# A gated cross-attention and mixture-of-experts block: the first batch on eight banks, xattn weights over a second queue, and q/k stacks filled from their own tiles

## The chip, the cores and the metric

The kernel runs on one core of one Trainium2 chip. A core has five engines that run side by side: TensorE (PE, matrix products, results in PSUM), VectorE (DVE), ScalarE (ACT), GpSimd (POOL) and SyncE (SP), which does nothing here but issue transfers. They meet only through semaphores. PSUM has eight banks of 128 x 512 fp32. The metric is the device time of one execution in microseconds; lower is better.

## The reference, cut to what matters

Four batches of 512 tokens with 256 features go through two parts: a gated cross-attention without a softmax (its result is a per-feature product), and a layer with a 16-head self-attention, a router and four experts.

```python
# part 1, per batch; xn = layernorm(x)
qh = (xn @ wq + bq) * gqw;  gq = sum_s(qh)
kh = (ctx @ wk + bk) * gq * gkw;  gk = sum_s(kh)
out = (ctx @ wv + bv) * gk + qh
x1 = x + tanh(g_xattn) * (out @ wo + bo)
# part 2; src = layernorm(x1)
q, k, v = src @ Wq + Bq, src @ Wk + Bk, src @ Wv + Bv          # 16 heads of 16
attn = softmax(q k^T / 4) v @ Wo + Bo
y = layernorm(src + attn) * ln1_g + ln1_b
e = floor(y @ router_w + router_b) mod 4                        # one expert per token
f = relu(y @ W1[e] + b1[e]) @ W2[e] + b2[e]
out = x1 + tanh(g_ffn) * layernorm_affine(y + f)
```

All is fp32. For accuracy q and k are kept as a high part and the rest ("lo"), and the scores are made from a stack of 48 rows per head: (q hi, q lo, q hi) against (k hi, k hi, k lo).

## The kernel before, in words

**Stages.** A lead does part 1 and the q, k, v projections of batch 0 (about 0 to 72 us). Then one loop over units u, 64 for each of the four batches, runs the attention of batch b and puts between its matmuls the part 1 and projections of batch b + 1 (up to about 420 us). A tail routes the tokens and runs the experts in slots of 256 tokens.

**A unit.** Unit u has one score matmul (`score`, L827, tile `sc`), one exponential on ACT (L549), and, 24 units ahead, one matmul for the row maxima (`score_for_maxima`, L818, tile `amax`) with a maximum on DVE (L686). Sixteen units are one group g of four heads of a batch; a batch has groups 0 to 3. Both matmuls read the stacks QS and KS. The first maxima matmul of group g waits for `stack_loaded[g]`; the first score of group g waits for the maxima of its sixteen rows, which DVE negates, splits and transposes (`mT`, L695) and SP moves through memory into two further rows of QS (`move_maxima`, L312 and L315).

**The queue of SP.** SP works through its transfers in program order, and each holds up those behind it until its own wait is over. For each batch `store_qk` (L291) writes the four q/k feature tiles HL to qk_dram, and `load_stack` (L303, L306) fills the stacks of one group from it with 12 transfers of 64 KB. A table `QUEUE` gives the unit at which each is written into SP's program: group 1 at -22, group 2 at -10, group 3 at 2, and the maxima of group g at 16 g - 8. Loads of batch b + 2 and of the expert weights (L352, L362) stand between. `load_stack` waits until the batch before has read the group's stacks.

**The lead.** The list `LEAD` gives its tasks: cT and xT (transposes of ctx and of the scaled x), gv (the sums behind gq and gk), Q, V, Y (part 1's three products), sT, q, k, v (part 2). All use two banks, side0 and side1, alternately; PE waits before it takes a bank until the task that had it before is evicted (`release`). Before the constants of DVE (L705 to L716) DVE waits for one semaphore `w_loaded` that counts all small loads and the four weights wq, wk, wv, wo (L700); PE's gv task waits for all twelve constants. Q is evicted to t1 (L607), and V combines it with gk (L612).

**Loads at the start.** SP issues everything: x, ctx, gates, the rows and columns, the four xattn weights (L330), then Wq, Wk, Wv and sixteen row pieces of Wo (L340), then x and ctx of batch 1. ACT waits for the gates, does one tanh, and then evicts cT. POOL waits for the gates too before it makes the first rstd.

Of the kernel before, what the change touches and what calls it, by code (L numbers as in the profile page):

```python
# [5 lines left out]
fp32 = mybir.dt.float32  # L6
# [8 lines left out]
def gated_block_kernel(nc, x, ctx, g_xattn, g_ffn, wq, bq, wk, bk, wv, bv, gqw, gkw, wo, bo,  # L15
# [23 lines left out]
    qk_dram = nc.dram_tensor("qk_dram", (4, 2, P, S), fp32, kind="Internal").ap()  # L39
# [6 lines left out]
    with es:  # L46
# [114 lines left out]
        pv = psum("pv", [P, 512])  # L161

# [6 lines left out]
        x_loaded, c_loaded, w_loaded, W_loaded, gates_loaded = sems("x_loaded c_loaded w_loaded W_loaded gates_loaded")  # L169
# [10 lines left out]
        m_loaded, qk_stored, stack_loaded = sems("m_loaded0 m_loaded1"), sems("qk_stored0 qk_stored1 qk_stored2 qk_stored3"), sems("stack0 stack1 stack2 stack3")  # L180
# [13 lines left out]
        W_LOADS, W_LOADS2 = 2 + 5 + 8 + 1 + 4, 3 + 16  # L194
        CONSTS = 12
# [12 lines left out]
        def rows_of(c, n):  # L208
# [19 lines left out]
                  -79: (("Q", 0),), -76: (("V", 0),), -73: (("Q", 1),), -71: (("V", 1),), -65: (("Y", 0),), -64: (("x1", 0),), -62: (("x1", 1),),  # L228
# [5 lines left out]
        QUEUE = {-117: ("load", 0), -42: ("store", 0), -39: ("store", 1), -37: ("store", 2), -34: ("store", 3),  # L234
                 -31: ("stack", 0), -22: ("stack", 1), -10: ("stack", 2), 2: ("stack", 3)}
# [12 lines left out]
        FIRST_PART = [("cT", 0), ("cT", 1), ("xT", 0), ("xT", 1), ("gv", 0), ("Q", 0), ("V", 0), ("Q", 1), ("V", 1), ("Y", 0), ("Y", 1)]  # L248
        LEAD = FIRST_PART + [("sT", 0), ("sT", 1), ("q", 0), ("q", 1), ("k", 0), ("k", 1), ("v", 0), ("v", 1)]

# [4 lines left out]
        def side_bank(task, i):  # L255

            return 1 if task in ("gv", "V") else 0 if task == "Q" else i % 2
# [8 lines left out]
        def release(task, n, b):  # L266
            return {"xT": (xT_done, b * 2 + n + 1), "cT": (cT_done, b * 2 + n + 1), "gv": (g4_done, b + 1),
                    "Q": (t1_done, b * 2 + n + 1), "V": (o_done, b * 2 + n + 1), "Y": (x1_done, b * 2 + n + 1),
                    "sT": (sT_done, b * 2 + n + 1), "q": (lo_done, b * 4 + n + 1), "k": (lo_done, b * 4 + n + 3),
                    "v": (v_done, b * 2 + n + 1), "O": (r_done, b * 2 + n + 1)}[task]  # L270

        def sp_program(sp):
# [11 lines left out]
            def store_qk(b, j):  # L284

                if j == 0:

                    for g in range(G):
                        wait(sp, stack_loaded[g], b * 192)
                sp.wait_ge(lo_done, b * 4 + j + 1)  # L290
                sp.dma_start(qk_dram[j, :, :, :].rearrange("h p n -> p h n"), HL[:, j, :, :].bitcast(fp32)).then_inc(qk_stored[j], 16)  # L291

            def load_stack(b, g, sides="qk"):

                if g == 0:
# [947 lines left out]
```

## Time and profile before

| what | value |
|---|---|
| median of 3 runs | 618.59 us (612.85, 618.59, 621.51) |
| the profiled execution | 614.73 us |
| its span, first to last instruction | 612.9 us |
| PE busy | 491.3 us, 80% of the span |
| DVE, ACT, POOL busy | 390.2, 244.7, 207.1 us |
| mean granted TensorE clock | 0.86 of 2.4 GHz |
| hardware transfers of the SP queue | 36432 packets, 38.84 MB |

The span is what the views show; the profiled execution's time is 1.8 us above it. "Idle before" in a row is the time that the engine waited right before the instruction, with what ended it. The granted clock is a share of 2.4 GHz; 0.5 is 1.2 GHz.

### The profile page before, as it was taken

The page shows a single profiled execution, that of the slowest core. Times are in us where ns is not written, and L with a number is a line of the kernel's source. Part 1 is how long each engine was busy: PE and PEld are TensorE (multiplying, and loading weights), DVE is VectorE, ACT ScalarE, POOL GpSimd, SP SyncE. Part 2 cuts the span into 40 slices and gives each one's busy share as a digit, 9 for nine tenths or more (in the row PEclk, how much of TensorE's full clock was granted, in tenths as well). Part 3 has the DMA queues.
Part 4 walks back from the last instruction along what each step waited for, and adds up shares of the span by engine and source line. Part 5 has one row for each costly group of instructions (what it writes and reads, how often), then busy time and mean ns, then how long its engine had stood idle before and what let it go on. Part 6 is the DMA issues. An engine that isn't in the chain of part 4 may idle for free. (4 is left out here: it accounts for less than half of the span.)

```text
span 612.9 us, 8282 instructions
## 1 busy us (share of the span) xinstructions
PE 491.3 (80%) x2528; PEld 281.8 (46%) x2528; DVE 390.2 (64%) x871; ACT 244.7 (40%) x482; POOL 207.1 (34%) x273
## 2 busy tenths in 40 slices
PE   2095769899898999999979798887239998988970
PEld 2053343434423433434332242223239988888970
DVE  2333446988768889679976779703885655655552
ACT  2000200465435456244654546447005555454440
POOL 3115110141101323403303248522144565455552
PEclk9997957999789899799995879655659999899995
DMA  5701844055334353632665840020021122111220
GB/s 145 164 0 38 282 129 67 3 198 180 84 78 121 114 196 93 139 102 58 152 187 140 176 112 3 2 70 1 1 68 35 51 61 58 45 52 40 64 54 25
DMA packets 41795, 55.00 MB, mean 90 GB/s; under 512 B 14367, under 2 KB 26143, under 8 KB 41760
## 3 DMA queue, kind: packets, MB, share of 16 engines
q1 hardware_dynamic: 36432, 38.84, 24.3%
q0 software_dynamic: 5328, 15.74, 8.5%
q8 instruction: 16, 0.26, 0.2%
q14 instruction: 19, 0.16, 0.1%
HBM read 37.51 MB, written 17.83 MB: 90 GB/s over the span
## 5 line engine op out<-in xcount | busy, mean ns | idle before, releaser
L549 ACT ACTIVATE probs<-sc 128x512 f32<-128x512 f32 x256 | 141.2, 595 | 178.0 <-PE sc L827 175.5
L686 DVE TENSOR_REDUCE mx<-amax 128x1 f32<-128x512 f32 x256 | 166.6, 677 | 58.9 <-PE amax L818 58.8
L827 PE MATMUL sc<-QS,KS 50*128 50x512 f32 x256 | 111.7, 520 | 15.3 <-ACT probs L549 12.2
L818 PE MATMUL amax<-KS,QS 48*128 48x512 f32 x256 | 110.4, 515 | 14.4 <-DMA KS<-qk_dram 8.5
L827 PEld LDWEIGHTS sc<-QS,KS 50*128 50x128 f32 x256 | 45.6, 210 | 121.2 <-issue 64.9
L818 PEld LDWEIGHTS amax<-KS,QS 48*128 48x128 f32 x256 | 43.9, 205 | 32.0 <-DVE mx L686 15.2
L1174 PE MATMUL amax<-W_hi,hid_hi 128*128 128x256 f32 x160 | 48.2, 301 | 3.8 <-DVE hid_lo L1074 3.6
L1174 PE MATMUL amax<-W_hi,hid_lo 128*128 128x256 f32 x160 | 46.6, 291 | 0.0
L1174 PE MATMUL amax<-W_lo,hid_hi 128*128 128x256 f32 x160 | 46.6, 291 | 0.0
L495 POOL TENSOR_TENSOR an<-av,rec 128x256 f32<-128x256 f32 x16 | 10.2, 637 | 106.8 <-DVE rec L675 106.7
L839 PE MATMUL pv<-probs,V1b 128*32 128x512 f32 x256 | 44.1, 769 | 1.4 <-ACT probs L549 1.2
L396 POOL TENSOR_SCALAR var_eps<-mv 128x4 f32<-128x4 f32 x12 | 2.8, 235 | 120.5 <-DVE mv L571 116.1
L758 PE MATMUL side<-xcT,w_first 128*128 128x512 f32 x64 | 40.8, 760 | 0.0
L839 PE MATMUL pv<-probs,V1a 128*32 128x512 f32 x256 | 39.6, 695 | 0.0
L991 ACT ACTIVATE t_a<-sc,b_col 128x256 f32<-128x256 f32 x40 | 19.3, 482 | 42.6 <-PE sc L1164 42.4
L930 POOL DMA_INDIRECT out_dram<-slot_z,ids_now x22 | 24.2, 1099 | 35.4 <-DVE slot_z L1114 32.0
L758 PE MATMUL side<-srcT,w_second 128*128 128x512 f32 x64 | 34.6, 667 | 0.8 <-ACT srcT L535 0.8
L1174 PEld LDWEIGHTS amax<-W_hi,hid_hi 128*128 128x128 f32 x160 | 32.0, 200 | 6.2 <-DVE hid_lo L1074 6.0
L1164 PE MATMUL sc<-slot_xT,W_hi 128*128 128x256 f32 x160 | 31.5, 292 | 1.5 <-DVE slot_xT L1068 1.5
L1174 PEld LDWEIGHTS amax<-W_lo,hid_hi 128*128 128x128 f32 x160 | 32.1, 200 | 0.0
L1174 PEld LDWEIGHTS amax<-W_hi,hid_lo 128*128 128x128 f32 x160 | 32.0, 200 | 0.0
L1074 DVE TENSOR_TENSOR hid_lo<-t_a,hid_hi 128x512 fp32r<-128x512 f32 x40 | 27.0, 690 | 6.0 <-ACT hid_hi L992 5.7
(180 smaller groups left out, 865.8 us busy)
## 6 DMA issues: line engine op xcount, KB each, us to landing
qk_dram<-HL SPq DMA_DIRECT2D x16, 512.0 KB, 4.6
QS<-qk_dram SPq DMA_DIRECT2D x96, 64.0 KB, 2.9
KS<-qk_dram SPq DMA_DIRECT2D x96, 64.0 KB, 3.0
W_sb<-in_L_ffn_W SPq DMA_DIRECT2D x8, 512.0 KB, 5.5
xc<-in_x SPq DMA_DIRECT2D x4, 512.0 KB, 3.6
xc<-in_ctx SPq DMA_DIRECT2D x4, 512.0 KB, 4.8
x_dram<-xc POOLq DMA_DIRECT2D x4, 512.0 KB, 3.4
res_dram<-t_a POOLq DMA_DIRECT2D x4, 512.0 KB, 5.4
```

Of the source, the lines that this page charges most:

```text
L495: nc.gpsimd.tensor_tensor(an[:, :, g % 2, :], av_v[:, :, 0:DH], rec[:, :].unsqueeze(2).broadcast_to([P, S // 32, DH]), ALU.mult).then_inc( ...
L549: nc.scalar.activation(probs[:, n % 8, c * 512:(c + 1) * 512], sc[c][:, :], ACT.Exp, scale=SCALE).then_inc(exp_done, 1)
L686: nc.vector.reduce_max(mx[:, to:to + 1], amax[m % 3][:, :], AX.X).then_inc(max_done, 1)
L758: last = nc.tensor.matmul(bank[:, :], w[:, k, c * P:(c + 1) * P], src[:, k, :], start=(k == 0), stop=(k == KD - 1))
L818: nc.tensor.matmul(amax[m % 3][:, :], QS[rows, pair, chunk * P:(chunk + 1) * P], KS[rows, pair, :], start=True, stop=True).then_inc(A_full, 1)
L827: nc.tensor.matmul(sc[c][:, :], KS[rows, pair, kc * P:(kc + 1) * P], QS[rows, pair, :], start=True, stop=True).then_inc(sc_full, 1)
L839: last = nc.tensor.matmul(pv[32 * hh:32 * hh + 32, :], V1[b % 2][:, kc, 8 * c + pair, :], probs[:, (2 * r + hh // 2) % 8, c * 512:(c + 1) ...
L930: nc.gpsimd.indirect_dma_start(out_rows, bass.IndirectOffsetOnAxis(ap=ids_now[:, a:a + 1], axis=0), slot_z[:, a, :], None, bounds_check=NT ...
L991: nc.scalar.activation(hid[:, q % 2, f % 2, :], hid_bank[f % 4], ACT.Relu, bias=bias)
L1074: nc.vector.tensor_tensor(low, hid[:, q % 2, :, :], high.bitcast(fp32), ALU.subtract).then_inc(hid_split, 1)
L1164: last = nc.tensor.matmul(hid_bank[f % 4], w, slot_xT[:, xp, k, :], start=((k, (xp, wp)) == steps[0]), stop=((k, (xp, wp)) == steps[-1]))
L1174: last = nc.tensor.matmul(amax[a][:, 0:D], (hid_hi, hid_lo)[xp][:, f, a * P:(a + 1) * P], w, start=(f == 0 and (xp, wp) == PARTS[0]), stop ...
```

## The change

- **Banks and order of the lead.** `LEAD` becomes cT, cT, V0, xT, xT, V1, gv, Q0, Q1, Y, Y and then sT, q, k, v; a table `LEAD_BANK` spreads batch 0 over all eight banks. V is now evicted first (gk V + C1 into oT), Q is added in place. Transposes of xT and sT wait tile by tile for their source.
- **Loads at the start.** ACT issues wv, wq, wk, wo and the two gates; SP the rest. `w_loaded` becomes seven semaphores. DVE needs only the rows gqw, gkw and the columns for its first six constants; the five that belong to part 2 are made after Q1. POOL's first rstd waits for gqw alone.
- **Stacks.** `qk_dram` and its stores are gone. `load_parts` copies from HL straight to the stacks: 6 transfers of 16 rows x 512 per side and feature tile, 24 of 32 KB per group in place of 12 of 64 KB. For group 0 of batch 0 SP issues q0, q1 and k0, and ACT issues k1. SP loads batch 1's x and ctx behind k0 now, ahead of the stacks of groups 1 to 3. ACT waits for all four groups of the batch before (no longer for the stores) when it overwrites HL.
- **Table of SP.** Group 0 at -39 (q) and -34 (k), group 1 at -22, group 2 at -6 (was -10), group 3 at 1 (was 2).
- Smaller: POOL's x1 store of batch 0 waits for all four src tiles and the constants.

The core of the diff:

```diff
-        FIRST_PART = [("cT", 0), ("cT", 1), ("xT", 0), ("xT", 1), ("gv", 0), ("Q", 0), ("V", 0), ("Q", 1), ("V", 1), ("Y", 0), ("Y", 1)]
+        LEAD = [("cT", 0), ("cT", 1), ("V", 0), ("xT", 0), ("xT", 1), ("V", 1), ("gv", 0), ("Q", 0), ("Q", 1), ("Y", 0), ("Y", 1),
+                ("sT", 0), ("sT", 1), ("q", 0), ("q", 1), ("k", 0), ("k", 1), ("v", 0), ("v", 1)]
+        LEAD_BANK = {"cT": (0, 1), "V": (4, 5), "xT": (2, 3), "gv": (6,), "Q": (7, 0), "Y": (1, 2),
+                     "sT": (3, 4), "q": (5, 6), "k": (7, 2), "v": (0, 1)}
...
-        QUEUE = {-117: ("load", 0), -42: ("store", 0), -39: ("store", 1), -37: ("store", 2), -34: ("store", 3),
-                 -31: ("stack", 0), -22: ("stack", 1), -10: ("stack", 2), 2: ("stack", 3)}
+        QUEUE = {-117: ("load", 0), -39: ("stack", (0, "q")), -34: ("stack", (0, "k")), -22: ("stack", (1,)), -6: ("stack", (2,)), 1: ("stack", (3,))}
...
-                sp.dma_start(qk_dram[j, :, :, :].rearrange("h p n -> p h n"), HL[:, j, :, :].bitcast(fp32)).then_inc(qk_stored[j], 16)
+            def load_parts(eng, b, g, side_of, c):
+                to = (QS, KS)[side_of == "k"]
+                for i, part in enumerate(((0, 1, 0), (0, 0, 1))[side_of == "k"]):
+                    at = 64 * c + DH * i
+                    for r in range(2):
+                        eng.dma_start(to[at:at + DH, 2 * g + r, :].bitcast(fp32),
+                                      HL[32 * g + DH * r:32 * g + DH * r + DH, c + 2 * (side_of == "k"), part, :].bitcast(fp32)).then_inc(stack_loaded[g], 16)
...
+            for side_of, c in (("q", 0), ("q", 1), ("k", 0)):
+                sp.wait_ge(lo_done, 1 + c + 2 * (side_of == "k"))
+                sp.wait_ge(stack_ready, 1)
+                load_parts(sp, 0, 0, side_of, c)
             load_batch(1)
...
         def act_program(act):
-            act.wait_ge(gates_loaded, 48)
+            for n, ap, s in (("wv", wv, wv_loaded), ("wq", wq, wq_loaded), ("wk", wk, wk_loaded), ("wo", wo, wo_loaded)):
+                act.dma_start(w_sb[n][:, :, :], ap.rearrange("(k p) n -> p k n", p=P)).then_inc(s, 16)
+            act.dma_start(gates[:, 0:1], g_xattn.partition_broadcast(P)).then_inc(gates_loaded, 16)
...
-            dve.wait_ge(w_loaded, W_LOADS * 16)
-            dve.wait_ge(gates_ready, 1)
+            dve.wait_ge(rows_s_loaded, 32)
+            dve.wait_ge(cols_loaded, 5 * 16)
```

The first place is PE in the lead of batch 0. Before, behind the transposes of cT, the rows are gv (xsum and csum), Q0, V0, Q1, V1, and Y:

```order
L753 MATMUL side1<-ident,xc 128x128 x4
L753 MATMUL side0<-ident,t_a 128x128 x4
L753 MATMUL side1<-ident,t_a 128x128 x4
L790 MATMUL side1<-xsum,w_first 128x1 x4
L790 MATMUL side1<-csum,w_first 128x1 x4
L758 MATMUL side0<-xcT,w_first 128x512 x2
L758 MATMUL side1<-xcT,w_first 128x512 x2
L758 MATMUL side0<-xcT,w_first 128x512 x2
L758 MATMUL side1<-xcT,w_first 128x512 x2
L766 MATMUL side0<-w_first,oC 128x256 x4
L766 MATMUL side1<-w_first,oC 128x256 x4
```

The same place after the change:

```order
L774 MATMUL side1<-ident,xc 128x128 x4
L779 MATMUL amax0<-xcT,w_first 128x512 x2
L774 MATMUL sc0<-ident,t_a 128x128 x4
L774 MATMUL sc1<-ident,t_a 128x128 x4
L779 MATMUL amax1<-xcT,w_first 128x512 x2
L811 MATMUL amax2<-xsum,w_first 128x1 x4
L811 MATMUL amax2<-csum,w_first 128x1 x4
L779 MATMUL pv<-xcT,w_first 128x512 x2
L779 MATMUL side0<-xcT,w_first 128x512 x2
L787 MATMUL side1<-w_first,oC 128x256 x4
L787 MATMUL sc0<-w_first,oC 128x256 x4
```

V0 and V1 (the two products that need ctx alone) moved ahead of gv, and no two tasks from V0 to Y0 share a bank.

The second place is SP in batch 1, from the maxima of group 0 (L312, L315) to those of group 1. Before, where the stack loads of group 3 lie between them and those of group 2 lie ahead:

```order
L303 DMA QS<-qk_dram 16x2x512
L306 DMA KS<-qk_dram 16x2x512
L312 DMA m_dram<-mT 4x32x32
L315 DMA QS<-m_dram 2x2x512 x2
L352 DMA W_sb<-in_L_ffn_W 128x1024
L303 DMA QS<-qk_dram 16x2x512
L306 DMA KS<-qk_dram 16x2x512
L303 DMA QS<-qk_dram 16x2x512
L306 DMA KS<-qk_dram 16x2x512
```

Ten more rows of L303 and L306 follow there, then:

```order
L303 DMA QS<-qk_dram 16x2x512
L306 DMA KS<-qk_dram 16x2x512
L352 DMA W_sb<-in_L_ffn_W 128x1024
L312 DMA m_dram<-mT 4x32x32
L315 DMA QS<-m_dram 2x2x512 x2
```

After the change (L310 and L313 are the maxima, L296 the stack pieces):

```order
L310 DMA m_dram<-mT 4x32x32
L313 DMA QS<-m_dram 2x2x512 x2
L345 DMA W_sb<-in_L_ffn_W 128x1024
L296 DMA QS<-HL 16x512 x12
L296 DMA KS<-HL 16x512 x12
L296 DMA QS<-HL 16x512 x12
L296 DMA KS<-HL 16x512 x12
L345 DMA W_sb<-in_L_ffn_W 128x1024
L310 DMA m_dram<-mT 4x32x32
L313 DMA QS<-m_dram 2x2x512 x2
```

Between the two moves of maxima stood 12 stack pieces and two weight loads; now 48 pieces and the same two loads do.

The third place is SP at the end of the lead, from the sixteen pieces of Wo to the first move of maxima, after the change:

```order
L335 DMA w_second<-in_L_ffn_Wo 16x256 x16
L296 DMA QS<-HL 16x512 x12
L296 DMA KS<-HL 16x512 x6
L286 DMA xc<-in_x 128x4x256
L288 DMA xc<-in_ctx 128x4x256
L296 DMA QS<-HL 16x512 x12
L296 DMA KS<-HL 16x512 x12
L296 DMA QS<-HL 16x512 x12
L296 DMA KS<-HL 16x512 x12
L296 DMA QS<-HL 16x512 x12
L296 DMA KS<-HL 16x512 x12
L310 DMA m_dram<-mT 4x32x32
```

Before, this place had x and ctx of batch 1, two stores, 6 pieces, two stores, 6 pieces, and 36 pieces for groups 1 to 3; now 18 pieces, x and ctx, and 72 pieces.

## Rows read from the trace of the kernel before

**Rows 1.** Stretch, busy us of PE, PEld, DVE, ACT, POOL, granted clock, DMA share, GB/s

```profile
180.00:260.00 80.00, 77.28 (x362) 33.04 (x360) 66.22 (x150) 39.50 (x74) 22.65 (x34) 0.91 0.44 127
```

**Rows 2.** Start, in order of time: start, us, engine, line, what, count, idle before

```profile
9.21 0.20 ACT L523 ACTIVATE tg<-gates 128x2 f32<-128x2 f32 x1 [7.20 <-DMA gates<-in_g_ffn]
...
24.54 0.88 DVE L705 TENSOR_SCALAR rows_bc<-rows_bc,tg 128x256 f32<-128x256 f32 x3 [12.11 <-DMA w_first<-in_L_xattn_wo]
...
30.85 1.84 PE L790 MATMUL side<-xsum,w_first 128*128 128x1 f32 x8 [16.34 <-DVE csum L591]
```

**Rows 3.** First batch, the same view

```profile
34.26 9.57 PE L758 MATMUL side<-xcT,w_first 128*128 128x512 f32 x16
...
43.87 0.75 DVE L612 SCALAR_TENSOR_TENSOR oC<-side,gk,t 128x512 f32<-128x512 f32 x1 [0.96 <-PE side L758]
...
52.45 2.19 DVE L628 TENSOR_SCALAR t_a<-xc,mv,rstd 128x256 f32<-128x256 f32 x4 [1.48 <-POOL rstd L398]
...
66.44 0.75 DVE L633 SCALAR_TENSOR_TENSOR HL<-side,cols,HL 128x512 fp32r<-128x512 f32 x1 [0.97 <-ACT HL L541]
...
71.71 1.40 DVE L567 BATCH_NORM_STATS2 stats<-xc 128x6 f32<-128x256 f32 x4
...
73.45 0.94 SPq L291 DMA_DIRECT2D qk_dram<-HL  x2
...
76.81 1.08 PE L753 MATMUL side<-ident,t_a 128*128 128x128 f32 x4 [4.30 <-DVE t_a L585]
77.80 2.65 SPq L306 DMA_DIRECT2D KS<-qk_dram  x6
...
82.34 0.79 PE L818 MATMUL amax<-KS,QS 48*128 48x512 f32 x2 [4.45 <-DMA KS<-qk_dram]
```

**Rows 4.** Stretch in which x and ctx land

```profile
2.00:5.00 3.00, 0.00 (x0) 0.00 (x0) 0.70 (x3) 0.01 (x1) 2.97 (x1) 1.00 0.98 338
```

**Rows 5.** SP's sixteen 16-row loads; landing times by transfer

```profile
20.86 7.51 SPq L340 DMA_DIRECT2D w_second<-in_L_ffn_Wo  x16
...
QS<-qk_dram SPq DMA_DIRECT2D x96, 64.0 KB, 2.9
...
xc<-in_x SPq DMA_DIRECT2D x4, 512.0 KB, 3.6
```

**Rows 6.** Maxima of the first group, and the first score

```profile
105.14 0.67 SPq L312 DMA_DIRECT2D m_dram<-mT  x1
107.18 1.29 SPq L315 DMA_DIRECT2D QS<-m_dram  x2
...
112.18 0.50 PE L827 MATMUL sc<-QS,KS 50*128 50x512 f32 x1
```

**Rows 7.** Waits of PE for the stack loads: us in total, times, longest

```profile
PE amax L818 <- DMA KS<-qk_dram: 8.5, 3, 4.5
```

**Rows 8.** Maxima of group 0 on SP; score of group 1, batches 1, 2, 3

```profile
180.53 0.55 SPq L312 DMA_DIRECT2D m_dram<-mT  x1
...
209.84 0.50 PE L827 MATMUL sc<-QS,KS 50*128 50x512 f32 x1
...
263.80 0.55 SPq L312 DMA_DIRECT2D m_dram<-mT  x1
268.14 1.26 SPq L315 DMA_DIRECT2D QS<-m_dram  x2
...
291.55 0.50 PE L827 MATMUL sc<-QS,KS 50*128 50x512 f32 x1
...
341.57 0.55 SPq L312 DMA_DIRECT2D m_dram<-mT  x1
...
348.17 0.49 PE L827 MATMUL sc<-QS,KS 50*128 50x512 f32 x1 [2.22 <-DMA QS<-m_dram]
...
367.14 0.47 PE L827 MATMUL sc<-QS,KS 50*128 50x512 f32 x1 [0.54 <-ACT probs L549]
```

**Rows 9.** Stretch behind a wait of PE of 2.8 us

```profile
323.00:340.00 17.00, 15.97 (x61) 4.55 (x60) 11.08 (x21) 7.56 (x14) 6.57 (x9) 0.51 0.64 125
```

More of the change, by code:

```diff
@@ L161, in gated_block_kernel @@
         pv = psum("pv", [P, 512])
+        BANKS = side + sc + amax + [pv]
         SEMS = {}
@@ L539, in side_work @@
                     act.wait_ge(qk_full, b * 4 + j + 1)
-                    wait(act, qk_stored[j], b * 16)
+                    for g in range(G):
+                        wait(act, stack_loaded[g], b * STACK)
+                    if b == 0 and j == 0:
+                        act.wait_ge(cols_loaded, 5 * 16)
                     nc.scalar.activation(HL[:, j, 0, :], bank[:, :], ACT.Identity, bias=cols[:, 3 + j // 2, i:i + 1]).then_inc(hi_done, 1)
@@ L552, in act_program @@
                 side_work(task, i, 0)
+            act.wait_ge(lo_done, 4)
+            act.wait_ge(stack_ready, 1)
+            for i, part in enumerate((0, 0, 1)):
+                for r in range(2):
+                    act.dma_start(KS[64 + DH * i:64 + DH * i + DH, r, :].bitcast(fp32), HL[DH * r:DH * r + DH, 3, part, :].bitcast(fp32)).then_inc(stack_loaded[0], 16)
             for u in range(BEGIN, END):
@@ L573, in side_work @@
             def side_work(task, i, b):
-                bank = side[side_bank(task, i)]
+                bank = BANKS[bank_of(task, i, b)]
                 if task == "x":
@@ new lines, in dve_program @@
+            side_work("cT", 0, 0)
+            side_work("cT", 1, 0)
+            dve.wait_ge(gates_ready, 1)
+            dve.wait_ge(bo_loaded, 16)
+            nc.vector.tensor_scalar(rows_bc[:, BO, :], rows_bc[:, BO, :], tg[:, 0:1], None, ALU.mult).then_inc(bo_ready, 1)
+            for task, i in (("gv", 0), ("V", 0), ("V", 1), ("Q", 0), ("Q", 1)):
+                side_work(task, i, 0)
+            later_constants()
+            side_work("Y", 0, 0)
+            for t in range(2):
+                side_work("x1", t, 0)
@@ L731, in dve_program @@
+            side_work("Y", 1, 0)
+            for t in range(2, TT + 1):
+                side_work("x1", t, 0)
+            for t in range(TT):
+                side_work("src", t, 0)
+            for v in V1:
+                nc.vector.memset(v[:, :, :, DH:2 * DH], 1.0).then_inc(v1_ready, 1)
+            for task, i in LEAD[LEAD.index(("q", 0)):]:
+                side_work(task, i, 0)
             for u in range(BEGIN, END + OVER):
@@ L748, in pe_program, with transposes @@
         def pe_program(pe):
-            before_side = [None, None]
-            def transposes(bank, src, c, full):
+            last_use = [None] * len(BANKS)
+            def transposes(bank, src, c, full, ready=None, b=0):
                 for t in range(TT):
+                    if ready is not None and c == 0:
+                        pe.wait_ge(ready, t + 1 + b * TT)
                     last = nc.tensor.transpose(bank[:, t * P:(t + 1) * P], src[:, t, c * P:(c + 1) * P], ident[:, :])
@@ L799, in side_work @@
                 elif task == "sT":
-                    pe.wait_ge(src_done, b * TT + TT)
-                    transposes(bank, t_a, i, sT_full)
+                    transposes(bank, t_a, i, sT_full, src_done, b)
                 elif task in "qk":
```

158 lines of the change are left out of this document (69 added, 89 removed), and 2 rows, old and new, of the table BLOCKS.

## The prediction

> **What bounds the kernel now.** I read the table of stretches first. In the attention loop PE is the bound: 77.28 us busy of 80, DVE 66.22, ACT 39.50 [rows 1]. Time that PE stands there is lost, and nothing gives it back. Then I read the timeline of the lead. It is a chain of waits instead: DVE stands 12.11 us until 24.54, for the last of the four weights in SP's queue, though its constants need none of them, and PE stands 16.34 us behind it, until gv at 30.85 [rows 2]. The end of the lead is a chain too: k0's low part is done at 66.44 + 0.75 = 67.2, its store goes out at 73.45, the loads of KS at 77.80, and the first maxima matmul starts at 82.34 [rows 3]. Last I read SP's queue, since the change doubles the stack transfers, and looked for what is queued behind them: x and ctx of the next batch, expert weights, and the maxima, on which PE's scores wait.
>
> **The front of the lead.** DVE's constants now wait for small loads only. PE has cT, V0, xT, V1 ahead of gv. ACT's tanh is at 9.21 [rows 2] and the two evictions of cT follow; the weights on the second queue share the transfer engines with x and ctx, so I place cT's end at 11. Eight transposes took about 1.9 us (four 1.08 at 76.81 [rows 3]; twice that is 2.2). The four tasks Q, V took 9.57 together, 2.4 each [rows 3]. So gv starts between 11 + 2.4 + 2 + 2.4 = 17.8 and about 20, since the first of them run at the low clock; I take 19. Against 30.85 that is 11.8 us. DVE's constants and sums took 6.3 us, 24.54 to 30.85 [rows 2], now less; they lie under V0 to V1 (11 to 19) if their loads land by 13, and each us later costs one. From gv to the last eviction of part 1 it now takes 43.87 + 0.75 - 30.85 = 13.8 [rows 2, 3], of which gv itself 34.26 - 30.85 = 3.4. With V already done it is 3.4, two products at 1.7 (the last step of the old chain, 0.96 + 0.75 [rows 3]) to 2.4, and one eviction: 7.7 (up to 9). Gain 6.1, together 17.9.
>
> The Trainium skill, DMA: Bandwidth & Descriptors, Issuing engines are not separate DMA queues, says that transfers of all issuing engines run on the same engines and a second issuer saves only issue time; that speaks against any gain from the second queue. The trace agrees: the stretch in which x and ctx land has share 0.98 at 338 GB/s [rows 4], full already. By it 1 MB of weights beside them makes ctx up to 3.1 us late, not the 1.5 us that my 11 holds, and the total would be 1.6 us higher.
>
> **From part 1 to the stacks.** Two of four statistics tasks slip in front of the second Y (0.7). The four src tiles took 2.19 from 52.45 while POOL worked beside them, and the transposes waited for all; tile by tile and with POOL held back I take 1.6 less. The q/k matmuls took their own time and no bank wait showed but small ones: 0.4. So k0's low part comes at 67.2 - 17.9 - 2.7 = 46.6 [rows 3]. POOL's held-back store of x1 is off this path, since SP asks for it only behind k0.
>
> SP issues a 16-row piece each 7.51 / 16 = 0.47 us [rows 5]. That is the nearest row to the new pieces, which also have 16 rows. k0's six pieces end at 49.4; x and ctx of batch 1 at 50.3; x lands 3.6 later [rows 5], at 53.0. ACT's six pieces of k1 (ready one product, 1.7 to 2.4, after k0) land by 49.0 + 2.8 + 2.9 = 54.7 [rows 5]. But in PE's order the first xT of batch 1 stands ahead of the first maxima, and from x's statistics to it took 76.81 - 71.71 = 5.1 [rows 3]; about the length of that xT is saved by its waiting tile by tile. So the first maxima is at 53.0 + 5.1 = 58.1. Before: 82.34. The chain through memory was 15 us behind k0, this one is 11.5, and **x of batch 1 is what is late next**, not the stacks.
>
> The first score was at 112.18 [rows 6], 29.8 behind the first maxima, so PE gets there at 88. SP: 72 pieces behind 50.3 end at 84.1, and only then the maxima move. That takes 2.0 for the store, 1.3 for the issue [rows 6], and a landing; in batch 3 it was 348.17 - 341.57 = 6.6 in all [rows 8]. I take 5.5 for it everywhere (bounds: 3.3, with no landing at all, and 6.6). The first score comes at 89.6, and the lead is worth **22.6 us**. A faster lead alone cannot better that, SP sets it.
>
> **In the loop.** PE's waits for KS, 8.5 in all with 4.5 the first, go in two later batches: the round through memory is gone, **gain 4.0** [rows 7]. Against it, between the maxima of group 0 and group 1 SP now has 48 pieces (48 x 0.47 = 22.6) where 12 stood. Group 1's maxima are needed by its first score:
> - batch 1: from 180.53 to 209.84 there are 29.3 us [rows 8]. Supply: the move of group 0, 3.3; 48 pieces and 2 weight loads, 23.5; the move of group 1, 5.5: 32.3. Late 3.0.
> - batch 2: 291.55 - 263.80 = 27.8 [rows 8]. Supply: 268.14 + 1.26 - 263.80 = 5.6, then 22.6, then 5.5: 33.7. Late 5.9.
> - batch 3: 367.14 - 341.57 = 25.6 [rows 8]. Supply 3.3 + 23.5 + 5.5 = 32.3. Late 6.7.
>
> That is **15.6 us lost**: PE's queue is in order, so all maxima and side matmuls behind that score stand too. If SP had no such queue ahead, the cost were nothing. The q eviction of ACT, which now waits for group 3's pieces, is covered: in batch 1 they have landed 3.3 + 23.5 + 2.9 = 29.7 behind 180.53, at 210.2, and q stands behind the first score of group 1 (209.84 plus its new wait). Group 2's pieces arrive within 1 us of their first use on both sides; I count nothing.
>
> A wait of 2.8 us was followed by 17 us at clock 0.51, with PE busy 15.97 [rows 9]; half speed costs at most 8.5 there. Two such waits go and three longer ones come. Bounds 0 and 8.5; I take **2 lost**, since the last batch runs partly on ACT.
>
> **The sum:** -22.6 - 4.0 + 15.6 + 2 = -9.0. The profiled execution's 614.73 becomes 605.7. It was 3.9 under the median 618.59; the same change on the median gives **609.6**, my number, 1.5% faster. The tail is not touched.
>
> **Rivals.**
> - *The group 1 waits don't come.* If SP issues pieces whose both ends are in SBUF faster, or the maxima are faster, only -22.6 - 4.0 or somewhat less is left: 592 to 596. It needs 15.6 / 3 = 5.2 us per batch, a piece at 0.36 in place of 0.47. Against it: six pieces of 64 KB took 2.65, 0.44 each [rows 3], so the pace hardly knows the size. For it: with the clock low PE needs the scores later. 0.18.
> - *The lead gives only half.* If ctx, gates and columns land late behind the weights, or the low clock covers V0 to gv, gv is at 23 or more; if x of batch 1 lands late among the stack pieces, a few more. With 12 instead of 22.6 it is 620. For it: the transfer engines are full [rows 4]. Against it: the wait for the weights alone was 12.11 [rows 2], and it is gone in any case. 0.16.
> - *Slower: copies within SBUF are slower than their issue.* 16 rows of 2 KB from the tile's partitions to the stack's, in one queue in order. If a piece holds the queue for more than its 0.47, SP's ring fills, and stacks and maxima are late in each group. 216 pieces lie on paths that bind (72, and 48 in three batches). 2% slower than 618.59 is 631; that takes 21 us more, 0.1 per piece, so it decides at 0.57 us per piece. At 0.8 it were 680. Against it: pieces of 64 KB, twice the bytes, landed in 2.9 [rows 5]. 0.08.
> - My forecast, with group 1's waits between 8 and 18 us: 0.58.
>
> **How the numbers follow.** A measurement tells 2% from no change, that is below 606.2 or above 631. My forecast's own range is 603 to 616; a third of it lies below 606.2: 0.20, with the first rival's 0.18 it is 0.38 faster. Slower 0.08. Same 0.54. The range goes from 593 to 621: it holds my forecast, half of the first rival and most of the second.
>
> **What would show it.** gv on PE near 19 us, k0's low part near 47, first maxima near 58, first score near 90 with a wait for QS from m_dram. SP without a gap from k0's pieces to about 84. In batches 1 to 3 a wait of PE for QS from m_dram at the first score of group 1, of 3, 6 and 7 us; no wait for KS. I am wrong if pieces do not go at 0.47, if those waits are under 2 us each, or if the clock falls for long after them.

## The result and the profile after

The changed kernel is slower: 668.12 us median (663.69 to 672.66, 4 runs) against 615.72 (608.94 to 621.51, 4 runs), a ratio of 1.098 with a 95% interval of 1.090 to 1.106. The profiled execution took 663.69 us with a span of 661.8. Forecast were 609.6 us and a range of 593 to 621; the true side had a chance of 0.08.

The lead did what it should up to k0. The timeline of the changed kernel, columns as in [rows 2]:

```profile
12.18 0.20 ACT L521 ACTIVATE tg<-gates 128x2 f32<-128x2 f32 x1 [6.48 <-DMA gates<-in_g_ffn]
...
20.28 0.95 PE L811 MATMUL amax<-xsum,w_first 128*128 128x1 f32 x8
...
45.82 0.75 DVE L640 SCALAR_TENSOR_TENSOR HL<-pv,cols,HL 128x512 fp32r<-128x512 f32 x1 [0.97 <-ACT HL L542]
...
60.05 1.94 PE L774 MATMUL side<-ident,xc 128*128 128x128 f32 x8 [9.82 <-DMA xc<-in_ctx]
...
63.65 0.80 PE L838 MATMUL amax<-KS,QS 48*128 48x512 f32 x2
...
106.09 0.79 PE L847 MATMUL sc<-QS,KS 50*128 50x512 f32 x1 [12.01 <-DMA QS<-m_dram]
```

gv starts at 20.28 (forecast 19, before 30.85 [rows 2]), k0's low part is done at 45.82 + 0.75 = 46.57 (forecast 46.6), the first maxima matmul is at 63.65 (forecast 58.1, before 82.34 [rows 3]). Then the gain is gone: the first score comes at 106.09 (forecast 89.6, before 112.18 [rows 6]), after 12.01 us in which PE stood for the maxima from m_dram. SP's queue over the same time shows why:

```profile
42.42 8.06 SPq L296 DMA_DIRECT2D QS<-HL  x12
50.58 3.73 SPq L296 DMA_DIRECT2D KS<-HL  x6
54.42 0.53 SPq L286 DMA_DIRECT2D xc<-in_x  x1
54.99 0.51 SPq L288 DMA_DIRECT2D xc<-in_ctx  x1
55.54 7.47 SPq L296 DMA_DIRECT2D QS<-HL  x12
...
93.71 7.54 SPq L296 DMA_DIRECT2D KS<-HL  x12
101.29 0.66 SPq L310 DMA_DIRECT2D m_dram<-mT  x1
```

SP has no gap from 50.58 on. Twelve pieces take 7.47 to 7.54 us here (7.87 once), **0.63 us a piece**, not the 0.47 that I took from Wo's pieces [rows 5]. The move of the maxima at 101.29 stands behind 72 of them. Before the 63.65 PE had already stood 9.82 us for ctx of batch 1, whose load SP reached only at 54.99, behind x.

The table of waits, for PE (us in total, times, longest):

```profile
PE sc L847 <- DMA QS<-m_dram: 38.6, 4, 12.0
...
PE amax L838 <- DMA KS<-HL: 25.5, 8, 5.6
```

Before, the loads of KS cost 8.5 us in three waits [rows 7] and the maxima 3.0 in two, the longer of 2.22 [rows 8]. Now it is 25.5 in eight and 38.6 in four. Four places carry 53 of these 64 us: the lead, and the stretch between the maxima of group 0 and the first score of group 1 in each later batch. The timeline there (L310 is the maxima's way out, the L838 rows are group 2's first maxima, the L847 rows group 1's first score):

```profile
177.14 0.60 SPq L310 DMA_DIRECT2D m_dram<-mT  x1
...
198.40 0.80 PE L838 MATMUL amax<-KS,QS 48*128 48x512 f32 x2 [4.26 <-DMA KS<-HL]
...
213.57 0.60 SPq L310 DMA_DIRECT2D m_dram<-mT  x1
...
219.46 0.79 PE L847 MATMUL sc<-QS,KS 50*128 50x512 f32 x1 [9.30 <-DMA QS<-m_dram]
...
296.63 0.80 PE L838 MATMUL amax<-KS,QS 48*128 48x512 f32 x2 [5.59 <-DMA KS<-HL]
...
316.52 0.79 PE L847 MATMUL sc<-QS,KS 50*128 50x512 f32 x1 [7.78 <-DMA QS<-m_dram]
...
392.27 0.80 PE L838 MATMUL amax<-KS,QS 48*128 48x512 f32 x2 [4.82 <-DMA KS<-HL]
...
406.73 0.61 SPq L310 DMA_DIRECT2D m_dram<-mT  x1
...
412.88 0.79 PE L847 MATMUL sc<-QS,KS 50*128 50x512 f32 x1 [9.53 <-DMA QS<-m_dram]
```

In batch 1 it is 219.46 - 177.14 = 42.3 us from one to the other, where the kernel before took 29.3 [rows 8]; PE stands 4.26 + 9.30 of it. In batch 2 the two waits are 5.59 and 7.78, in batch 3 4.82 and 9.53.

The transfer engines are not what is full. The first row is the stretch in which SP issues pieces and hardly anything else, the second the landing time of a piece:

```profile
60.00:95.00 35.00, 32.01 (x84) 16.58 (x84) 22.11 (x44) 2.57 (x6) 4.70 (x7) 0.67 0.22 51
...
QS<-HL SPq DMA_DIRECT2D x192, 32.0 KB, 2.0
```

DMA share 0.22 at 51 GB/s, and 2.0 us from issue to landing, less than the 2.9 of the pieces from memory, which carry 64 KB [rows 5].

Spans add up so. From the first score to the end it is 661.8 - 106.1 = 555.7, before 612.9 - 112.2 = 500.7: the loop and tail lost 55.0, the lead gained 6.1, together +48.9. The loop alone, from the first score to the last (columns as in [rows 1]; the first row is the kernel before), with the stretch behind the first score below it for each kernel:

```profile
112.18:417.90 305.72, 280.99 (x1293) 109.24 (x1292) 231.15 (x492) 154.07 (x284) 91.05 (x116) 0.87 0.41 111
106.09:467.90 361.81, 294.71 (x1292) 111.50 (x1292) 234.18 (x491) 154.21 (x284) 90.75 (x116) 0.79 0.28 76
...
112.00:129.00 17.00, 15.88 (x87) 6.67 (x85) 15.75 (x36) 11.38 (x21) 7.51 (x11) 1.00 0.10 34
106.00:123.00 17.00, 16.14 (x58) 5.66 (x58) 13.00 (x30) 7.62 (x14) 5.07 (x7) 0.50 0.01 3
```

The loop is 56.1 us longer. PE stands 67.1 us of it where it stood 24.7, and is busy 13.7 us longer with the same matmuls, at a granted clock of 0.79 for 0.87. Behind the wait of 12.01 us the clock is 0.50, and 58 matmuls keep PE busy for 16.14 us; in the kernel before 87 took 15.88.

### The profile page after: what moved, and what is told of

It is laid out like the page before. It is cut to its first block and busy times, and to the rows that moved or that the text cites. A ratio compares the mean times of both kernels' runs of the same rounds, so it can differ in the third digit from the quotient of the medians.

```text
span 661.8 us, 8466 instructions
## 1 busy us (share of the span) xinstructions
PE 500.3 (76%) x2528; PEld 279.4 (42%) x2528; DVE 392.8 (59%) x871; ACT 244.4 (37%) x482; POOL 206.9 (31%) x273
## 5 line engine op out<-in xcount | busy, mean ns | idle before, releaser
L847 PE MATMUL sc<-QS,KS 50*128 50x512 f32 x256 | 119.7, 556 | 51.3 <-DMA QS<-m_dram 38.6
L838 PE MATMUL amax<-KS,QS 48*128 48x512 f32 x256 | 115.0, 556 | 29.5 <-DMA KS<-HL 25.5
L847 PEld LDWEIGHTS sc<-QS,KS 50*128 50x128 f32 x256 | 49.4, 227 | 165.5 <-issue 73.3
L838 PEld LDWEIGHTS amax<-KS,QS 48*128 48x128 f32 x256 | 46.1, 223 | 43.8 <-DMA KS<-HL 28.2
L859 PE MATMUL pv<-probs,V1b 128*32 128x512 f32 x256 | 46.9, 815 | 1.2 <-ACT probs L550 1.2
L859 PE MATMUL pv<-probs,V1a 128*32 128x512 f32 x256 | 43.8, 764 | 0.0
L1012 ACT ACTIVATE t_a<-sc,b_col 128x256 f32<-128x256 f32 x40 | 19.3, 484 | 40.7 <-PE sc L1185 34.6
L1195 PEld LDWEIGHTS amax<-W_hi,hid_hi 128*128 128x128 f32 x160 | 30.5, 191 | 8.4 <-DVE hid_lo L1095 7.9
L779 PE MATMUL side<-xcT,w_first 128*128 128x512 f32 x52 | 31.6, 716 | 0.0
L1195 PEld LDWEIGHTS amax<-W_lo,hid_hi 128*128 128x128 f32 x160 | 30.6, 191 | 0.0
L1185 PEld LDWEIGHTS sc<-slot_xT,W_hi 128*128 128x128 f32 x160 | 25.8, 198 | 2.7 <-issue 1.9
```

What stands on the lines that cost most here:

```text
L779: last = nc.tensor.matmul(bank[:, :], w[:, k, c * P:(c + 1) * P], src[:, k, :], start=(k == 0), stop=(k == KD - 1))
L838: nc.tensor.matmul(amax[m % 3][:, :], QS[rows, pair, chunk * P:(chunk + 1) * P], KS[rows, pair, :], start=True, stop=True).then_inc(A_full, 1)
L847: nc.tensor.matmul(sc[c][:, :], KS[rows, pair, kc * P:(kc + 1) * P], QS[rows, pair, :], start=True, stop=True).then_inc(sc_full, 1)
L859: last = nc.tensor.matmul(pv[32 * hh:32 * hh + 32, :], V1[b % 2][:, kc, 8 * c + pair, :], probs[:, (2 * r + hh // 2) % 8, c * 512:(c + 1) ...
L1012: nc.scalar.activation(hid[:, q % 2, f % 2, :], hid_bank[f % 4], ACT.Relu, bias=bias)
L1185: last = nc.tensor.matmul(hid_bank[f % 4], w, slot_xT[:, xp, k, :], start=((k, (xp, wp)) == steps[0]), stop=((k, (xp, wp)) == steps[-1]))
```

## The experiments

Each run stands beside the kernel before on the same chip, whose median was 613.4 to 615.8 us. Numbers of one run alone are called so. In the diffs ... stands for lines that are left out.

**1. The new lead without the new stacks.** Lead, banks, loads and semaphores of the change; the stacks through qk_dram with the old table.

```diff
-            for side_of, c in (("q", 0), ("q", 1), ("k", 0)):
-                sp.wait_ge(lo_done, 1 + c + 2 * (side_of == "k"))
...
-                load_parts(sp, 0, 0, side_of, c)
-            load_batch(1)
+            load_batch(1)
+            for side_of, js in (("q", (0, 1)), ("k", (2, 3))):
+                for j in js:
+                    store_qk(0, j)
...
+                load_stack(0, 0, side_of)
```

> The changed kernel with one part undone: banks, order and loads of the lead stay new, the stacks are filled as before (four stores to memory, 12 pieces of 64 KB per group). Theory A (all of the loss is SP's issue time for 24 pieces of 0.63 us per group): the loop takes what it took before, 500.7 us from the first score to the end, and the lead gives about 20 us, so about 595 us; waits of PE for KS and QS as before, some 11 us. Theory B (the new lead or the eight banks cost something later, such as the clock): the loop stays longer than 510 us and the total is above 605. A lead that is worth nothing gives 615.

Measured: 592.59 us, ratio 0.968 (0.955 to 0.981). The lead is worth about 21 us by itself. That is theory A's 595 and not theory B's 605. (The profiled execution, 602.8, lay 10 above the median, and took 507.5 from the first score at 93.5 to the end, between the two theories; the rows below are of the lead.)

```profile
41.87 0.39 SPq L288 DMA_DIRECT2D xc<-in_x  x1
...
63.16 0.79 PE L846 MATMUL amax<-KS,QS 48*128 48x512 f32 x2 [7.05 <-DMA KS<-qk_dram]
...
PE amax L846 <- DMA KS<-qk_dram: 12.2, 3, 7.0
```

The first maxima are at 63.16, the same as in the changed kernel (63.65), although k goes through memory and PE waits 7.05 us for it. There x of batch 1 is issued at 41.87, in the changed kernel at 54.42, behind eighteen pieces. So the direct stacks did not bring the start forward: what the round through memory had cost, the wait for x then cost.

**2. The old lead with the new stacks.** The reverse.

```diff
-                    store_qk(0, j)
...
-                load_stack(0, 0, side_of)
...
+                    load_parts(sp, 0, 0, side_of, c)
```

> The other part alone: the old lead with the new stacks (24 pieces of 32 KB per group from the tiles, none through memory, all issued by SP). Theory A: first maxima near 82 as before, then 72 pieces at 0.63 us before the first move of maxima, so the first score near 131, and from there the 555.7 us of the changed kernel: about 689 us, 12% slower. Theory B (the loss comes from the new lead and stacks together): clearly less than 670.

Measured: 688.32 us, ratio 1.131 (1.119 to 1.143). The stacks and their table alone lose 75 us; the lead gives 20 of them back (688.3 - 668.1). The timeline (SP's queue, PE) and the waits:

```profile
124.49 0.66 SPq L303 DMA_DIRECT2D m_dram<-mT  x1
...
129.38 0.79 PE L816 MATMUL sc<-QS,KS 50*128 50x512 f32 x1 [18.40 <-DMA QS<-m_dram]
...
PE sc L816 <- DMA QS<-m_dram: 42.8, 4, 18.4
```

The maxima move goes out at 124.49 and the first score comes at 129.38, 18.40 us late. It is what theory A said (689). Both halves of the change are thereby priced, and the loss is in the stacks.

**3. Pieces of the same shape, but out of memory.** Stores to qk_dram as before, then 24 pieces of 16 x 512 per group; only group 0 of batch 0 straight from the tiles.

```diff
+                        sp.dma_start(to[at:at + DH, 2 * g + r, :].bitcast(fp32),
+                                     qk_dram[c + 2 * (side_of == "k"), part, 32 * g + DH * r:32 * g + DH * r + DH, :]).then_inc(stack_loaded[g], 16)
...
-                        load_parts(sp, b, g, side_of, c)
+                        load_pieces(b, g, side_of, c)
```

> The changed kernel with the same 24 pieces of 16 x 512 per group, but read from memory behind the four stores of before (only group 0 of batch 0 still comes from the tiles). If the price of 0.63 us belongs to pieces with both ends in SBUF, these are issued at 0.47 and the total is near my forecast, 600 to 615. If it belongs to any piece of one head, they stay at 0.63 and the total stays near 668.

Measured: 643.98 us (one run). SP's queue, landing, waits:

```profile
71.42 5.51 SPq L315 DMA_DIRECT2D KS<-qk_dram  x12
...
KS<-qk_dram SPq DMA_DIRECT2D x180, 32.0 KB, 1.8
...
PE sc L872 <- DMA QS<-m_dram: 26.1, 5, 9.9
```

Twelve pieces take 5.51 us, 0.46 each: that is my 0.47, and it belongs to pieces that come from memory. The 0.17 us on top belong to pieces with both ends in SBUF. But with 0.46 I had expected 600 to 615 here, and that missed: 26.1 us of waits for the maxima and 22.8 us for KS are left, and 5% to the kernel before. This kernel also has the stores and SP's waits for them (in batch 0 SP issues nothing from 58.8 to 65.7), so how long the changed kernel itself would take at 0.47 stays open.

**4. The order of the table.** Group 3's stack at unit 9, behind the maxima of group 1, in place of unit 1 ahead of them.

```diff
-                 -6: ("stack", (2,)), 1: ("stack", (3,))}
+                 -6: ("stack", (2,)), 9: ("stack", (3,))}
```

> The changed kernel with one number changed: the stack of group 3 stands at unit 9 in SP's table, behind the maxima of group 1, not at 1. If only the order in the queue costs, the waits of PE for QS from m_dram in batches 1 to 3 (9.3, 7.8, 9.5 us) go, and the total falls by about 25 to 640 or less. If SP is full (96 pieces at 0.63 are 60 us of a batch, with the moves of maxima 73 to 79 of about 80), the waits move to KS for groups 2 and 3 and the gain is under 12.

Measured: 649.71 us (one run). The waits for the maxima fall from 38.6 to 19.3 (12.8 of it in the lead), those for KS only from 25.5 to 22.1. The gain of 18 lies between the two expectations. With the maxima ahead the stacks themselves are late, since the queue is nearly full either way, and a third wait shows:

```profile
ACT HL L542 <- DMA KS<-HL: 13.5, 2, 7.6
```

ACT must not overwrite HL before group 3's pieces have landed, and PE's scores then wait for ACT (24.3 us, before this edit 12.6). The prediction had called this eviction covered; with the table as changed it is, with group 3 eight units later it is not.

**5. Half the bytes per piece.** Columns 0 to 255 of each piece only; the kernel leaves out the other half, which stays at a constant, so its scores are not those of the reference.

```diff
-                        eng.dma_start(to[at:at + DH, 2 * g + r, :].bitcast(fp32),
...
+                        eng.dma_start(to[at:at + DH, 2 * g + r, 0:256].bitcast(fp32),
...
```

> The changed kernel, but each of the 24 pieces per group carries only columns 0 to 255 of the 512 (16 KB in place of 32 KB); the other half of each stack's columns is left at a constant, so half of the score inputs are not computed values. Count, rows and queue are the same. Theory A, 0.63 us is the price of issuing one transfer with both ends in SBUF: pace of 12 pieces 7.4 to 7.6 us, time stays 655 to 670. Theory B, the price is that of bytes (each piece waits for the one before to move): 12 pieces take about 3.8 to 4.5 us, SP has 15 to 20 us spare per batch, the waits of the first scores for QS from m_dram shrink to under 10 us in all, and the time is 615 to 630.

Measured: 656.56 us (one run). SP's queue, and the stretch of pieces:

```profile
79.09 7.54 SPq L296 DMA_DIRECT2D KS<-HL  x12
...
60.00:95.00 35.00, 32.10 (x84) 16.64 (x84) 22.63 (x48) 2.57 (x6) 4.70 (x7) 0.66 0.10 26
```

Twelve pieces of 16 KB take 7.54 us, to the hundredth what pieces of 32 KB took, with the DMA share down to 0.10. The price is per transfer and not per byte; theory B is out. From the first score to the last this kernel took 366 us, the changed kernel 362; its lower total comes from the tail, which has 144 matmuls of L1186 into sc where the changed kernel has 160.

**6. Half the count for the same bytes.** The two heads of a pair now lie on the same 16 partitions of two feature tiles (the columns of Wq and Wk are permuted once by ACT), so one transfer of 64 KB takes both. SP's table is the changed kernel's. The edit does one thing more: x and ctx of batch 1 go out behind q's pieces, ahead of k's.

```diff
-                    for r in range(2):
-                        eng.dma_start(to[at:at + DH, 2 * g + r, :].bitcast(fp32),
...
+                    eng.dma_start(to[at:at + DH, 2 * g:2 * g + 2, :].bitcast(fp32),
+                                  HL[64 * c + DH * g:64 * c + DH * g + DH, 2 * (side_of == "k"):2 * (side_of == "k") + 2, part, :].bitcast(fp32)).then_inc(stack_loaded[g], 16)
...
+                if side_of == "q":
+                    load_parts(sp, 0, 0, side_of, 1)
+                    load_batch(1)
```

> The changed kernel, with the two heads of a pair in two feature tiles on the same 16 partitions (columns of Wq and Wk permuted once in the lead, biases loaded in that order), so that one transfer takes both heads: 12 pieces of 64 KB per group, both ends still in SBUF, and no memory in between. Theory A, the count of issues on SP's queue is the cost: at 0.63 us a piece a batch takes 30 us of SP, less than the 12 pieces and stores of before would need at once, the waits for QS from m_dram are gone but for under 5 us in all, first score at about 93 to 96, time 590 to 603. Theory B, the cost lies in the bytes within SBUF (a piece of 64 KB then costs about 1.26 us): pace of 6 pieces 7.5 us, waits as in the changed kernel, time 655 to 670. Theory C, data straight from the tiles are late for another reason than issue: pace as in A, but waits for KS or QS above 20 us, time above 620.

Measured: 590.24 us, ratio 0.969 (0.952 to 0.987): 78 us less than the changed kernel. SP's queue and the landing time:

```profile
71.30 3.77 SPq L297 DMA_DIRECT2D KS<-HL  x6
...
82.28 0.59 SPq L311 DMA_DIRECT2D m_dram<-mT  x1
...
QS<-HL SPq DMA_DIRECT2D x96, 64.0 KB, 2.4
```

Six pieces of 64 KB take 3.77 us, 0.63 each once more. SP is through with the stacks of batch 0 at 75.1 and waits for the maxima, which go out at 82.28; of PE's waits for the maxima 4.8 us in three are left, for KS 1.4 in one. The earlier x is a small part of it: the first maxima are at 61.00, 2.65 us sooner than in the changed kernel. Data straight from the tiles are fine, and so is 0.63 us, if there are 48 of them in a batch and not 96.

**7. Straight pieces only where the chain waits.** Group 0 of batch 0 from the tiles, all others through memory with 12 pieces and the old table.

```diff
             for side_of, c in (("q", 0), ("q", 1), ("k", 0)):
...
                 load_parts(sp, 0, 0, side_of, c)
-            load_batch(1)
+                if (side_of, c) == ("q", 0):
+                    load_batch(1)
+            for j in range(4):
+                store_qk(0, j)
```

> The new lead with group 0 of batch 0 filled straight from the tiles (24 pieces, 6 of them on ACT's queue) and every other group through memory as before (12 transfers of 64 KB, the old table). x and ctx of batch 1 go out behind q0's pieces. Theory A, straight pieces are worth their price only where the chain waits for them (k0 to the first maxima): first maxima at 58 to 61 (63.16 with new lead and old stacks), first score at 90 to 94, time 1 to 4 us under that kernel, about 589 to 592. Theory B, x of batch 1 or the queue behind sets the start and not the stacks: no difference to new lead and old stacks within 0.5%, 591 to 596.

Measured: 588.12 us, ratio 0.966 (0.949 to 0.983), with the first maxima at 59.41 and the first score at 89.60. Both times are about those of theory A (58 to 61, 90 to 94); the total is not distinguishable from run 1 (592.59, 585.38 to 602.80).

**8. The same pieces, with the maxima on another queue.** The changed kernel; the move of each group (a store and two loads) is issued by POOL at the same units.

```diff
-        QUEUE.update({16 * g - 8: ("maxima", g) for g in range(G)})
+        GPSIMD.update({16 * g - 8: ("maxima", g) for g in range(G)})
```

> The changed kernel, but the moves of the maxima through memory are issued on POOL's queue at the same units, so they no longer stand behind stack pieces. The 96 pieces per batch stay on SP's queue at 0.63 us each, 60.5 us of about 80. Theory A, the maxima were late because they stand behind 48 pieces in one queue: PE's waits for QS from m_dram fall from 38.6 us to under 8, the first score comes at 92 to 96 in place of 106.1, KS waits stay or shrink, and the time is 600 to 620. Theory B, SP has no room for the pieces wherever the maxima stand: waits for QS go, but waits for KS at the first maxima of groups grow by as much, above 45 us, and the time stays above 640. Theory C, POOL is late with its own work and takes SP's place as the late one: waits for QS from m_dram above 20 us, with POOL behind on an, x1 or the residual.

Measured: 602.39 us (602.11 and 602.67), ratio 0.987 (0.975 to 0.998). The waits, POOL's rows for the store to m_dram, and the stretch 180 to 260 (columns as in [rows 1]):

```profile
PE sc L848 <- DMA QS<-m_dram: 8.4, 4, 4.3
...
L478 POOL DMA_DIRECT2D m_dram<-mT x16 | 12.5, 779 | 51.3 <-DVE mT L704 45.6 <-issue 5.7
...
180.00:260.00 80.00, 77.25 (x375) 32.04 (x368) 70.40 (x150) 40.85 (x76) 31.22 (x48) 0.97 0.38 107
```

This is the sharpest of the runs. All 96 pieces per batch stay where they were, at 0.63 us, and 66 us of the time are gone because 48 small transfers no longer stand behind them. The waits for the maxima fall from 38.6 to 8.4 and those for KS from 25.5 to 2.3, so theory B is out; the first score is at 93.48. PE is busy 77.25 of 80 us as before the change [rows 1]. SP has room for the pieces, about 61 of 80 us; it has none for something urgent behind them.

**9. The weights on SP's queue again.** Run 1's kernel; wv, wq, wk, wo are issued by SP behind the columns.

```diff
+                load_weight(n, ap, s)
...
-                act.dma_start(w_sb[n][:, :, :], ap.rearrange("(k p) n -> p k n", p=P)).then_inc(s, 16)
```

> New lead and old stacks (593 us), but wv, wq, wk and wo are issued on SP's queue again, behind gqw, gkw and the five columns; banks, task order and the separate semaphores stay. Theory A, the gain at the front comes from the order of the tasks and from not waiting for the weights, and the second queue saves 2 us of issue at most: V0 starts at 13.5 to 15.5 (13.50 with two queues), gv at 20 to 22.5 (20.28), time 591 to 597. Theory B, the second queue carries it: V0 behind 17, gv behind 25, time 598 or more.

Measured: 598.75 us (594.72 and 602.77), within run 1's spread; the total alone would also fit theory B (598 or more), the places do not. PE in the front:

```profile
12.55 3.45 PE L787 MATMUL amax<-xcT,w_first 128*128 128x512 f32 x4 [2.25 <-DMA w_first<-in_L_xattn_wv]
...
18.43 0.95 PE L819 MATMUL amax<-xsum,w_first 128*128 128x1 f32 x8
```

V0 starts at 12.55 and gv at 18.43, no later than with two queues (13.50 and 20.28; in runs 1, 6 and 10 gv was at 20.06, 19.52 and 18.93). ACT's tanh came at 7.62 here and at 12.18 with the weights ahead of the gates; what was won there V0 then waited for wv (2.25). The second queue brought nothing that shows. That leaves the order of tasks, the eight banks and the waits that name what they need as the source of the front's gain; no run takes these apart.

**10. x of batch 1 earlier.** Run 6's kernel without POOL's wait for all four src tiles before it stores x1, behind which the buffer of x comes free.

```diff
-                    pool.wait_ge(src_done, TT)
```

> The paired tiles with 12 pieces of 64 KB, and POOL's store of x1 in batch 0 no longer waits for all four src tiles, so x of batch 1 can be loaded earlier. Theory A, x of batch 1 sets the first maxima (61.0 with the wait): first maxima at 57 to 60, first score at 89 to 91.5, time 585 to 589. Theory B, POOL beside DVE slows the four src tiles by as much (the reason for the wait), or SP's q pieces stand ahead anyway: k0's low part 0.5 to 1.5 us later, no gain, 588 to 592.

Measured: 585.54 us, ratio 0.961 (0.951 to 0.970). SP's load of x, and PE:

```profile
47.68 0.53 SPq L288 DMA_DIRECT2D xc<-in_x  x1
...
58.81 0.80 PE L852 MATMUL amax<-KS,QS 48*128 48x512 f32 x2
...
88.76 0.50 PE L861 MATMUL sc<-QS,KS 50*128 50x512 f32 x1
```

The first maxima are at 58.81 (61.00 in run 6) and the first score at 88.76 (92.33). The places moved as theory A says. Theory B's premise came too: beside POOL the four src tiles took 2.20 us, 1.38 in run 6, but that did not undo the gain. The 4.7 us in the total are about what the runs of either kernel differ among themselves (4.5 and 5.9).

**11. All of it together.** Runs 6, 9 and 10 in one kernel.

```diff
+                load_weight(n, ap, s)
...
-                act.dma_start(w_sb[n][:, :, :], ap.rearrange("(k p) n -> p k n", p=P)).then_inc(s, 16)
```

> All that helped, together: paired tiles with 12 pieces of 64 KB per group, x of batch 1 early, and the four xattn weights on SP's queue again behind the columns. Theory A, the front gains what one queue gave with the old stacks (gv 18.4 in place of 20.3) and the end of the lead follows it: first maxima 57 to 58.5, first score 87 to 88.5, time 582 to 586. Theory B, x of batch 1 and the maxima of group 0 set the first score and it stays at 88.8: no difference to the two queues, 584 to 588.

Measured: **583.79 us, ratio 0.956 (0.950 to 0.963)**, better than both kernels, and not distinguishable from run 10: gv was at 20.25 and the first maxima at 61.05 here, so the 2 us that run 9 showed at gv did not come again. They are spread between executions.

## Why the prediction was wrong, by its steps

**What bounds the kernel** was read rightly: PE in the loop, a chain in the lead, and SP's queue as the thing to look at. The queue did decide.

**The front.** gv at 20.28 for 19. ACT's tanh came at 12.18 (before 9.21 [rows 2]), and in run 9, where the gates are ahead of the weights, at 7.62. PE's first transposes, which wait for ctx, came at 7.99 for 5.91, 2.1 later (1.5 in my sum); but in run 9, with the weights issued from 8.60 on, they came at 8.36, so that the weights beside ctx were the cause is not shown. cT's end was at 13.35 for 11, and from V0 to gv it took 6.8, the sum without its allowance for the low clock. k0's low part came at 46.57 for 46.6, in part by luck: gv was 1.3 late, and from gv to the last eviction it took 6.2 (20.28 to 26.45) for 7.7. Run 1 shows the lead worth 21 us (forecast 22.6), but with the old stacks; in the changed kernel the first score came 6.1 sooner.

**The price of a piece** is the step that failed. "SP issues a 16-row piece each 7.51 / 16 = 0.47 us. That is the nearest row to the new pieces" [rows 5]: nearest in shape, but Wo comes from memory. Run 3 measured 0.46 for pieces of memory and the changed kernel 0.63 for pieces of SBUF; runs 5 and 6 show the same 0.63 at a half and at double the bytes. My rows held loads from memory alone, and the range took no other price. It is not the whole miss: the account below adds two terms that I had put at nothing or too small, the pieces of q and of the other groups in the same queue, and the clock.

**The lead.** Forecast: SP through its 72 pieces at 84.1. It was at 101.25. 72 x 0.16 = 11.5 of the 17.2 are the price. Of the rest, 4.0 is the start and 1.0 the price of k0's own six: k0's pieces could begin at 50.58 and not at 46.6, since the twelve of q stood ahead of them until 50.48. I had let k0's pieces start when their data were ready, and not when the queue was. Even at 0.47 q's twelve would have ended at 48.1. The same start made x late: SP asked for it at 54.42, not 49.4, its statistics began at 58.23 for 53.0, and the first maxima came at 63.65 for 58.1. That x of batch 1 is what is late next was right. The move itself then took 4.8 where I had 5.5. So the first score came 17.2 - 0.7 = 16.5 late, 106.1 for 89.6.

**Group 1's first score.** The form of the sum was right, supply against demand between two moves. With 48 pieces at 0.63 in place of 0.47 (7.7 more each) its 3.0, 5.9 and 6.7 become 10.7, 13.6 and 14.4, 38.7 in all. PE's waits in these three stretches were 13.6, 13.4 and 14.4, 41.3 in all, for 15.6 forecast. What I had not seen is that the first third shows as a wait for KS: "Group 2's pieces arrive within 1 us of their first use" failed in each batch (4.26, 5.59, 4.82).

**Waits for KS** were to go, a gain of 4.0. Besides those three there were five more, 10.9 us: pieces of the other groups came late too, for which I had counted nothing.

**The clock.** Forecast were 2 lost, with bounds 0 and 8.5. Measured, PE was busy 13.7 us longer with the matmuls of the loop (280.99 to 294.71, granted clock 0.87 to 0.79). Three long waits, I had reasoned, replace two; there were twelve. Behind the four for the maxima the clock was at 0.50, 0.59, 0.50 and 0.50 (106 to 123, 219 to 224, 316 to 322, 413 to 419). Run 8, with the same pieces and hardly any of these waits, had PE busy 283.2 us over its loop at 0.85, so 11.5 of the 13.7 went with the waits. One execution of each is profiled, but all four of the changed kernel had a mean clock of 0.798 to 0.813 and those of the kernel before beside the experiments 0.832 to 0.880.

**The account.** The loop's 56.1 us are +41.3 for the three stretches, +10.9 for the other KS waits, +13.7 for the clock, less 4.1 and 3.0 for the kernel before's later waits for KS and the maxima, less 2.7 in waits for other engines. With -6.1 for the lead and -1.1 for the tail that is the span's 48.9. Against the forecast of -9.0 the lead missed by 16.5, the group 1 stretches by 25.7, the KS waits by 10.8 and the clock by 11.7; small gains elsewhere take 6.8 off.

**The rivals.** The one that came was the one with 0.08: a piece that holds the queue for longer than 0.47, deciding at 0.57. Its reason was off by a word, since it looked at the landing of copies within SBUF, which is quick (2.0 us), and not at their issue. Its slope was also too flat: 216 pieces by 0.16 is 35 us and gives 644, and 668 was measured. The pieces beyond these 216 (all of groups 0 and 2, the eighteen of the first group) were not free once the queue was full, and the clock took 11.7 of the 24 that this slope misses. The chance was too small because the only evidence against it, pieces of 64 KB landing in 2.9 [rows 5], was again of pieces out of memory, and of landing.

The Trainium skill, DMA: Bandwidth & Descriptors, Issuing engines are not separate DMA queues, says that issuing from several engines saves only the issue time, "which is usually small relative to the DMA itself". Its first half agrees with run 9, where a second queue brought nothing. The second half does not carry over to this kernel: 0.63 us of issue stands beside 2.0 us to landing, landings of one queue overlap while its issues don't (a piece every 0.63 us), and run 8 gained 66 us by giving 48 small transfers another issuer.

## What to carry to other kernels

A queue that issues transfers is an engine with its own busy time: count issues, price each by a row with the same kind of source and destination, and add it up per period, 96 x 0.63 = 61 us of 80 here, before you trade few large transfers for many small ones. Ask next what urgent, tiny transfer stands behind the bulk; moving it to an issuer with time to spare, or laying out the data so that one transfer takes two pieces, was worth 66 and 78 us here (the 78 with x of batch 1 earlier as well). A stall costs more than its own length when the clock falls with it: 13.7 us beside 42.4 of standing here. And a chain starts when the queue is free, not when the data are.

## What the runs showed of the hardware

- A transfer with both ends in SBUF took 0.63 us of issue on SP's queue at 16, 32 and 64 KB alike (7.54 / 12, 7.54 / 12, 3.77 / 6), one of the same shape and destination from memory 0.46 (5.51 / 12 in run 3). On ACT's queue the six of k1 took 3.81 us, also 0.63. Why the two kinds differ the runs don't show; the two-row loads of the maxima, out of memory but in fine strides, also took 0.62 to 0.65 each, so the source alone may not be what counts.
- Memory traffic fell from 37.5 to 24.9 MB read and from 17.8 to 9.4 MB written, and the kernel became 10% slower, with the transfer engines at a share of 0.28 in the loop (before 0.41). Run 5, with half the bytes per piece, kept the pace and the waits (37.5 us for the maxima, 21.6 for KS).
- The same small transfers cost POOL 0.55 (load) and 0.78 us (store) each, 30 us in all over the kernel (run 8), and did not hold PE up there: it was busy 77.25 of 80 us from 180 to 260.
- Behind waits of PE of 7.8 to 12.0 us the granted clock was 0.50 to 0.59 in the next stretch. How long differed: 17 us behind the first (0.50 from 106 to 123), but 1.00 again from 224 to 229 behind the one that ended at 219.46.
- DVE's four src tiles took 2.19 us while POOL worked beside them (run 10: 2.20) and 1.38 us while POOL stood (changed kernel, run 6).
